# GpSimd makes the gate's sigmoid and its sum with the experts' bias; VectorE keeps the rest of the choice of experts

## What is computed

```
x = x + attention(layernorm(x))                  # 16 heads mixed within a token, rope
x = x + cross_attention(layernorm(x), cond)      # 2048 queries x 2048 keys, 16 heads, quantised q, k, v and weights
x = x + experts(layernorm(x))                    # 8 experts, the best 2 per token, and a shared one

scores = sigmoid(xt @ gate.T)                    # (tokens, 8)
_, sel = top_k(scores + expert_bias, 2)
top_scores = take_along_axis(scores, sel)        # scales what is routed to each expert
```

## Time and profile before

| | us |
|---|---|
| median of 3 runs | 1030.79 (1030.5 to 1033.09) |
| the profiled execution | 1029.04 |
| its span, first to last instruction | 1027.3 |
| DVE busy | 908.6 (88%) |
| POOL busy | 746.1 (73%) |
| ACT busy | 737.0 (72%) |
| PE busy | 706.5 (69%) |
| the DMA queue that SP issues on, share of 16 engines' span | 83.9% |
| L1169, in all (16 instructions) | 29.9 |
| L1167, in all (16 instructions) | 10.4 |
| L1180, in all (16 instructions) | 8.1 |

### The profile page before, as it was taken

The page is one execution under the profiler, slowest core; times in us unless marked ns, Lnnn a source line. Parts: engine busy times, 40 slices in busy tenths (PEclk is TensorE's granted clock), DMA queues, the critical chain, the costliest instruction groups (busy, mean ns, idle before and its releaser), DMA issues. The chain is left out here.

```text
span 1027.3 us, 21133 instructions
## 1 busy us (share of the span) xinstructions
PE 706.5 (69%) x6995; PEld 385.7 (38%) x7072; DVE 908.6 (88%) x1841; ACT 737.0 (72%) x989; POOL 746.1 (73%) x728
## 2 busy tenths in 40 slices
PE   6965547676685867676876757686767677675664
PEld 4543223334252434343433424243434344242333
DVE  3897858999989899999999999999999999999952
ACT  2644565868788787878787887878786878878752
POOL 6688988779697879798896969797979879720000
PEclk9986877889897888898797979788989879798965
DMA  6011775989989897989898998979797989999891
GB/s 234 1 42 50 149 133 108 189 134 187 167 170 169 148 175 143 183 143 188 131 195 158 173 173 145 195 135 196 137 187 134 193 142 183 178 164 184 164 170 26
DMA packets 574018, 156.01 MB, mean 152 GB/s; under 512 B 567251, under 2 KB 571862, under 8 KB 573526
## 3 DMA queue, kind: packets, MB, share of 16 engines
q1 hardware_dynamic: 573910, 154.67, 83.9%
HBM read 9.93 MB, written 2.10 MB: 12 GB/s over the span
## 5 line engine op out<-in xcount | busy, mean ns | idle before, releaser
L1135 DVE TENSOR_SCALAR_CACHE_REDUCE score<-ps_score,q_neg 128x1024 f32<-128x1024 f32 x512 | 636.4, 1277 | 18.5 <-PE ps_score L1459 17.1
L824 ACT ACTIVATE prob<-score,exp_bias 128x2048 uint16<-128x2048 f32 x256 | 512.2, 2002 | 61.5 <-DVE exp_bias L1145 60.1
L1459 PE MATMUL ps_score<-keys,queries 128*128 128x512 bf16 x947 | 351.3, 455 | 230.6 <-DVE score L1135 218.1
L1459 PEld LDWEIGHTS ps_score<-keys,queries 128*128 128x128 bf16 x1024 | 72.7, 103 | 408.0 <-DVE score L1135 380.6
L527 POOL TENSOR_TENSOR product<-hs_exp,v_tok 128x1024 f32<-128x1024 f32 x64 | 149.4, 2347 | 31.0 <-ACT hs_exp L789 30.8
L534 POOL TENSOR_TENSOR product<-product 128x512 f32<-128x512 f32 x128 | 159.4, 1262 | 0.0
L527 POOL TENSOR_TENSOR product<-qk_rot 128x1024 f32<-128x1024 f32 x64 | 150.1, 2347 | 0.3 <-POOL qk_rot L520 0.2
L1489 PE MATMUL ps_pv<-prob_t,values 128*32 128x128 f16 x4096 | 73.8, 228 | 19.6 <-DMA prob_t<-prob 19.2
L545 POOL TENSOR_TENSOR product<-product 128x512 f32<-128x512 f32 x64 | 81.1, 1276 | 5.9 <-POOL product L534 5.9
L1489 PEld LDWEIGHTS ps_pv<-prob_t,values 128*32 128x32 f16 x4096 | 63.0, 101 | 50.0 <-issue 50.0
L1317 PE MATMUL ps<-routed_both,w 128*128 128x128 bf16 x512 | 45.7, 251 | 25.2 <-DMA routed_both<-routed_both 23.5
(11 more groups left out here) (124 smaller groups left out, 1141.1 us busy)
## 6 DMA issues: line engine op xcount, KB each, us to landing
prob_t<-prob SPq DMA_TRANSPOSE x256, 4.6
prob_t<-in_w SPq DMA_DIRECT2D x3, 1024.0 KB, 4.8
x_in<-in_x SPq DMA_DIRECT2D x16, 128.0 KB, 3.0
score<-in_cond_t SPq DMA_DIRECT2D x4, 512.0 KB, 6.6
out<-x_out SPq DMA_DIRECT2D x16, 128.0 KB, 2.6
w_qkv<-in_w_qkv SPq DMA_DIRECT2D x1, 768.0 KB, 4.1
early<-in_w_kv SPq DMA_DIRECT2D x1, 512.0 KB
w_s<-in_w_s SPq DMA_DIRECT2D x3, 128.0 KB
```

What stands on the lines that cost most here:

```text
L824: act.activation(prob[:, s, :].bitcast(U16), score[:, s, :], ACT.Exp, bias=exp_bias[:, s:s + 1], scale=-1.0, accum_out=prob_sum[:, t.par, ...
L1135: dve.tensor_scalar(score[:, s, HALF * i:HALF * i + HALF], ps_score[:, score_slot(t.count(H, h), i)].rearrange("p b k -> p (b k)"), q_neg[ ...
L1459: mm = pe.matmul(ps_score[:, score_slot(n, i), b, :], queries[:, t.par, h // 2, h % 2, :], keys[:, h // 2, k0:k0 + KEYS], start=True, stop ...
```

## The change

`choose` on DVE loses its first two instructions and the wait for ACT's tanh; it now begins by waiting for the second increment of `gate_chain`. POOL gets a function `gate_sums(m)`, placed behind `ln_scale(1, n)` and ahead of `score_products(2, a)`. It waits for the tanh, and makes the same two results with a tensor_scalar and a tensor_tensor (instead of a scalar_tensor_tensor with factor 1). `sem_inc(settled, 1)` is a semaphore increment that nobody waits for.

```diff
@@ gpsimd
+            def gate_sums(t):
+                sig, biased = gate[:, 0, :], gate[:, 1, :]
+                pool.wait_ge(gate_tanhed, t.count(1, 1))
+                pool.sem_inc(settled, 1)
+                if (due := t.due(6)) is not None:
+                    pool.wait_ge(gate_chain, due)
+                    pool.sem_inc(settled, 1)
+                pool.tensor_scalar(sig, gate_tanh[:], 0.5, 0.5, ALU.mult, ALU.add).then_inc(gate_chain, 1)
+                pool.wait_ge(gate_chain, t.count(6, 1))
+                pool.sem_inc(settled, 1)
+                pool.tensor_tensor(biased, sig, b_expert[:], ALU.add).then_inc(gate_chain, 1)
...
                 if n.exists():
                     ln_scale(1, n)
+                if m.exists():
+                    gate_sums(m)
                 if a.exists():
                     score_products(2, a)
@@ vector, choose
-                dve.wait_ge(gate_tanhed, t.count(1, 1))
-                dve.tensor_scalar(sig, gate_tanh[:], 0.5, 0.5, ALU.mult, ALU.add).then_inc(gate_chain, 1)
-                dve.wait_ge(gate_chain, t.count(6, 1))
-                dve.scalar_tensor_tensor(out=biased, in0=sig, scalar=1.0, in1=b_expert[:], op0=ALU.mult, op1=ALU.add
-                                         ).then_inc(gate_chain, 1)
                 dve.wait_ge(gate_chain, t.count(6, 2))
                 dve.max(best, biased).then_inc(gate_chain, 1)
```

## The result

The changed kernel takes 1019.98 us (median of 4 runs, 1015.19 to 1022.9) against 1031.0 for the kernel before, measured beside it: a ratio of 0.9885, 95% interval 0.9841 to 0.9929. Measured a second time it took 1017.4 us, and the ratio was 0.9850 (0.9822 to 0.9878). It is faster by 1.1 to 1.5%.

A forecast was written before the change was run, and what follows sets the result against it. DVE, busy 88%, was taken as the bound, with a DMA loop of nearly the same length; -13 x 1.4 + 0.5 = -17.7 us, taken as -17, gave 1012.0 profiled and 1014 as median; range 998 to 1030.

The forecast's parts named there:

- The likeliest case: Half of DVE's gain passes to the total, the rest becomes waiting for PE; chance 0.50, 1005 to 1022 us.
- The hold on the ports: DVE's L1167, L1169 and L1180 wait for POOL's instruction to end: medians 0.72, 2.26, 0.58 us against 0.17 at least.
- The choice: DVE's choice, L1167 to L1180, takes 1.4 us instead of 4.12; 2.6 us gained in each of thirteen choices.
- `hs` next late on POOL: POOL's work up to `hs` comes 2.0 us later, so DVE may wait some tenths for it at its maximum.
- The DMA loop decides: The loop from head 3 through turn_routed's landing takes 54.7 us, longer than DVE's 53.5: 1.4 us gained a tile.
- the stretch from head 3 to turn_routed: SP's issues of ten heads' transposes and the load of x, up to turn_routed's issue: from 28.6 to 27.4 us.
- The base of the loop: In one tile before the change, head 3 to landing 35.02 us, landing to next head 3 21.57, together 56.59.
- The size: Thirteen tiles at 1.4 us less each, plus 0.5 at the end: -17.7 us, taken as -17.
- The end: The last choice is on the path, and POOL needs 0.95 us there in all: +0.5 us.
- L1180 free: Bound on the gain in a choice if L1180 met no POOL product and took 0.17 us: 3.5 us.
- The rule against elementwise work on GpSimd: GpSimd about 2 times slower with two inputs; for 8 elements about 0.1 us a tile, leaving the sum the same.

The follow-up runs named there:

- e1: The kernel before with the sigmoid written to PSUM bank 7 instead of SBUF, POOL left as it was: 1020.8 us, ratio 0.9887.
- e6: The changed kernel with gate_sums placed behind score_products(2, a) on POOL instead of ahead of it: 1016.5 us, ratio 0.9840.
- e4: The changed kernel with SP's load of x two heads later, right behind turn_routed: 1009.0 us, ratio 0.9770.
- e4b: The kernel before with SP's load of x two heads later, right behind turn_routed: 1030.1 us, ratio 0.9991.
- e8: The kernel before with the sigmoid in PSUM and SP's load of x right behind turn_routed: 1006.5 us, ratio 0.9747.
- e3: The changed kernel with the transposes of heads 5 and 8 halved from tile 1 on, so results are stale: 1010.9 us, ratio 0.9795.
- e10: e8 with PE's experts(0, 0, o) behind both halves of head 0's scores instead of between them: 998.6 us, ratio 0.9670.

## Why the prediction was right, point by point

The forecast was 1014 with 1005 to 1022 as its own range; the median is 1020.0 and, measured again, 1017.4. The likeliest case was the one that happened, by the mechanism that was named. The size of the gain was overrated: 17 us forecast, 11.0 and, by the second ratio, 15 measured.

- *The hold on the ports.* The three instructions wait for the end of POOL's instruction: shown by e1.
- *The choice.* A gain of 2.6 us a choice was taken, and the means of 13 choices give 2.7. The sum takes POOL 0.20 us and not 0.27. POOL waited 1.4 to 2.2 us for the tanh in the 13 tiles, not 1.0: waking took 0.28 us, not 0.2, and POOL reached the wait earlier against ACT.
- *`hs` next late on POOL.* Predicted as some tenths, measured 0.3 to 0.5 us in 11 tiles. I gave it no cost, and in the changed kernel e6 shows none.
- *The DMA loop decides.* Shown by e4 against e4b. The mis-sized term is the stretch from head 3 to turn_routed. It was to fall from 28.6 to 27.4 us; over twelve tiles it fell from 28.7 to 28.0. The sum hid part of this by luck: the landing came 5.3 us behind the issue and not 5.8, so head 3 to landing is 33.3 us (32.2 to 34.5) where 33.2 was worked out. With 21.8 us back to the next head 3 the tile is 55.1 us, not 54.7.
- *The base of the loop.* The tile that I read, 35.02 us to the landing and 21.57 back, was at the long end. The mean of the kernel before is 33.9 and 22.0. The DMA loop was close behind DVE's path there and not ahead of it: e4b takes the load out of the loop, and the tile stays (56.3 us).
- *The size.* A tile gave 1.0 us and not 1.4. The span fell by 14.5 us: 4.1 ahead of the first choice, 12.0 in the next twelve tiles, 0.9 behind the last choice, and the last three tiles, for which I had put no term, took 2.5 us more (140.0 to 142.5). They took longer in e1 (144.1), e4 (143.1) and e8 (144.4) too, and no run tells why. The rest of the distance to the median is that the profiled execution lay 4.8 us under its median, where that of before lay 1.75 under.
- *The end.* The last choice cost 0.44 us from the tanh's end (1008.27) to DVE's maximum (1008.71) and now costs 0.89 (994.23 to 995.12): +0.45 where +0.5 was forecast.
- *Slips in the working.* 28.57 us over eleven items (ten heads and the load of x) are 2.6 us an item, not over 2.7; and with L1180 free the gain is 3.4 us, not 3.5. Neither enters the sum.
- *The rule against elementwise work on GpSimd* (the Trainium skill, "GPSIMD Engine Reference", section "Engine selection"). It did not matter here: 0.20 us against 0.17 for 8 elements, far from 2 times.

What stays open: what binds the changed kernel once the queue is lighter (e3). POOL's delay, the 0.8 us that its choice is still longer than with PSUM, and DVE's waits for PE at head 8, which rose from 23.8 to 31.0 us, are all candidates, and no run parts them.

## What to carry to other kernels

When a tiny VectorE instruction takes ten times its shortest duration, lay its row beside GpSimd's. If both end together, as here in 13 of 13 choices, it is held and not slow, and moving an operand to PSUM or the instruction to another engine frees it. Before crediting the whole gain to the total, look for a second loop of nearly the same length, here a queue of DMAs issued without a gap whose landing the other engines wait for; a waiting engine in front of shared work (the products of the experts between two halves of scores) is where the gain disappears. Edits to the two loops add up to more than their parts: the PSUM operand alone brought 1.1% and the load of x alone nothing, both together 2.5% (e8), and with PE's order as well 3.3% (e10). Take the base of such a loop from the mean of many tiles: the one tile read here was 1.1 us longer to the landing than the mean.

## What the runs showed of the hardware

The dependence on phase was larger than I had thought: beside POOL's products L1190 took from 0.49 to 1.70 us in one execution, by where in the product it began, and always ended with it.

The hold works the other way too. In the kernel before, POOL's L466, one element a partition and 0.22 us at its median, took 2.08 us once, when DVE ran two large tensor_scalar instructions from SBUF to SBUF; it began beside the first and ended with the second, at 76.88 against 76.85:

```profile
74.52 2.33 DVE L1052 TENSOR_SCALAR prob_t<-score 128x2048 f16<-128x2048 f32 x2
74.80 2.08 POOL L466 TENSOR_SCALAR var_eps<-mean_var 128x1 f32<-128x1 f32 x1 [3.15 <-DVE mean_var L1080]
```

The instructions with 8 elements a partition on GpSimd took 0.196 to 0.205 us in all 32 cases of the changed kernel. The executions of a kernel spread: the changed one's four over 7.7 us (1015.19 to 1022.9), fifteen of the kernel before over 9.8 (1026.19 to 1035.96), so a single execution can't tell 5 us.
